# Recurrent stage of a pre-norm decoder layer: output projection of batches two to four as three rounded products of halves in place of fp32 matmuls

## The reference, cut to what matters

```python
def _min_gru(x, Wz, bz, Wh, bh):
    k = x @ Wz + bz
    log_z = -jax.nn.softplus(-k)
    log_coeffs = -jax.nn.softplus(k)
    log_tilde_h = _log_g(x @ Wh + bh)
    a_star = jnp.cumsum(log_coeffs, axis=1)
    log_h = a_star + _logcumsumexp(log_z + log_tilde_h - a_star, axis=1)
    return jnp.exp(log_h)
out_fwd = _min_gru(x, Wz_f, bz_f, Wh_f, bh_f)
out_bwd = _min_gru(x_rev, Wz_b, bz_b, Wh_b, bh_b)
concat = jnp.concatenate([out_fwd, out_bwd], axis=2)
return concat @ W_out + b_out
...
x = x + _L0_attn_ref(_layernorm(x, axis=-1), ...)
x = x + _L0_xattn_ref(_layernorm(x, axis=-1), ctx_1024, ...)
x = x + _L0_ffn_ref(_layernorm(x, axis=-1), ...)
```

## Time and profile before

| what | value |
|---|---|
| median of 3 runs | 404.35 us (404.19 to 405.8) |
| profiled execution, span | 403.8 us |
| profiled execution, its own time | the page gives none beside the span; the lowest timed run is 404.19 us |
| instructions | 7801 |
| PE busy | 395.0 us, 98% |
| DVE busy | 300.1 us, 74% |
| ACT busy | 237.8 us, 59% |
| POOL busy | 215.9 us, 53% |
| output projection | from 29.84 us (first batch) to 93.6 us (last batch) |

### The profile page before, as it was taken

One profiled execution on the slowest core, in us unless ns is written; L12 is line 12 of the kernel. 1 busy time (PEld: TensorE's weight loads), 2 busy tenths in 40 slices (PEclk: granted clock), 3 DMA queues, 4 the chain that ended last, 5 costly groups with the idle time before them and its releaser, 6 DMA issues.

```text
span 403.8 us, 7801 instructions
## 1 busy us (share of the span) xinstructions
PE 395.0 (98%) x2584; PEld 367.1 (91%) x2584; DVE 300.1 (74%) x1093; ACT 237.8 (59%) x519; POOL 215.9 (53%) x209
## 2 busy tenths in 40 slices
PE   8999999999999999999999999999999999999877
PEld 7878888899999999999999999999788899999766
DVE  5797768786757867476864848572986989899996
ACT  3886859454764466464545434342557977779462
POOL 1788999764385333153430300000166858989993
PEclk9999999999999999999999999999999969999999
DMA  7900213004434312233211000000100000000102
GB/s 226 310 2 1 83 55 102 8 11 128 128 89 121 118 30 59 58 84 104 65 47 30 2 0 2 1 2 2 27 1 2 0 2 2 28 28 27 41 28 67
DMA packets 19992, 21.38 MB, mean 53 GB/s; under 512 B 3180, under 2 KB 16624, under 8 KB 19952
## 3 DMA queue, kind: packets, MB, share of 16 engines
q1 hardware_dynamic: 18832, 19.96, 16.5%
q10 hardware_dynamic: 1120, 0.92, 0.7%
HBM read 18.78 MB, written 2.10 MB: 52 GB/s over the span
## 4 chain that ended last, share of the span: by engine, by line
PE 80%; POOL 12%; DVE 4%; issue 3%; DMA 1%; ACT 0%; SPq 0%; DVEq 0%; POOLq 0%; ACTq 0%
PE keep_pQ L75 11%; PE keep_pQ L76 11%; PE keep_pQ L77 11%; POOL ffn_prod L1258 9%; PE context_pA L1051 6%; PE context_pA L1053 6%; PE context_pA L1052 6%; PE context_pR L1085 6%; PE context_pR L533 3%; PE context_pA L533 3%; POOL ffn_near L1326 2%; PE ffn_pK L1807 2%; PE context_pR L75 2%; PE context_pR L77 2%; PE context_pR L76 2%
## 5 line engine op out<-in xcount | busy, mean ns | idle before, releaser
L899 DVE TENSOR_TENSOR att_pTl<-context_pR,att_pTh 128x512 fp32r<-128x512 f32 x64 | 36.9, 586 | 29.8 <-ACT att_pTh L811 29.5
L811 ACT ACTIVATE att_pTh<-context_pR 128x512 fp32r<-128x512 f32 x64 | 32.1, 514 | 40.1 <-PE context_pR L1085 40.1
L1258 POOL TENSOR_TENSOR ffn_prod<-ffn_first,ffn_near 128x1024 f32<-128x1024 f32 (+1 forms) x29 | 54.1, 1885 | 2.1 <-DVE ffn_first L1684 2.1
L851 ACT ACTIVATE att_prob<-keep_pQ,att_nmax 128x1206 f32<-128x1206 f32 x16 | 20.3, 1269 | 35.9 <-DVE att_nmax L935 35.8
L930 DVE TENSOR_REDUCE att_mx<-keep_pQ 128x1 f32<-128x402 f32 x64 | 34.5, 564 | 6.9 <-PE keep_pQ L77 6.6
L1837 PE MATMUL ffn_pT<-keep_ident,ffn_prod 128*128 128x128 f32 x240 | 30.5, 283 | 3.7 <-POOL ffn_prod L1258 3.7
L1837 PEld LDWEIGHTS ffn_pT<-keep_ident,ffn_prod 128*128 128x128 f32 x240 | 28.6, 148 | 5.8 <-DVE ffn_hT L1717 4.8
L786 POOL TENSOR_TENSOR keep_rstd<-att_ve,keep_mhalf 128x4 f32<-128x4 f32 x3 | 3.0, 1007 | 55.9 <-DVE att_ve L989 55.9
L1085 PE MATMUL context_pR<-keep_ident,att_prob 128*128 128x128 f32 (+1 forms) x208 | 31.8, 272 | 0.2 <-DVE att_pTl L899 0.2
L1051 PE MATMUL context_pA<-att_pTh,att_cNh 128*128 128x256 f32 (+1 forms) x104 | 31.0, 298 | 0.0
L1051 PE MATMUL context_pA<-att_pTh,context_cNh 128*128 128x256 f32 (+1 forms) x104 | 30.9, 297 | 0.0
(11 more groups left out here) (336 smaller groups left out, 1300.3 us busy)
## 6 DMA issues: line engine op xcount, KB each, us to landing
keep_raw<-in_ctxT SPq DMA_DIRECT2D x24, 256.0 KB, 2.7
keep_raw<-in_ctx SPq DMA_DIRECT2D x24, 256.0 KB, 3.0
out<-keep_x SPq DMA_DIRECT2D x16, 128.0 KB, 1.7
keep_x<-in_x SPq DMA_DIRECT2D x3, 512.0 KB, 9.9
gru_wout<-in_W_out SPq DMA_DIRECT2D x1, 512.0 KB, 8.7
keep_raw<-in_fWq SPq DMA_DIRECT2D x2, 256.0 KB
keep_raw<-in_ctxT SPq DMA_DIRECT2D x8, 32.5 KB, 3.1
keep_raw<-in_ctx SPq DMA_DIRECT2D x4, 65.0 KB
```

The lines of the kernel that those rows point to most:

```text
L811: act.activation(to, bank, ACT.Copy).then_inc(bank_high, 1)
L899: dve.tensor_tensor(to, bank, half(it, 0, n)[0].bitcast(F32), ALU.subtract).then_inc(bank_free, 1)
L1258: return eng.tensor_tensor(prod[:, i % PB, a:b].rearrange("p h (i j) -> p h i j", j=KEYS), (factor if factor is not None else first[:, n % ...
```

## The change

The output projection of the first batch stays in fp32. Those of batches two to four are made of halves. `state_high` (ACT) rounds each unit's state into `hh[b]`, `state_low` (DVE) subtracts in place (`hTl` lies over `hT`), and `halved_output` makes twelve products for a tile in place of four fp32 matmuls. W_out is halved once, at unit 6 on ACT and unit 7 on DVE, in place too, behind the first batch's four tiles. The tiles of batches two and three move one projection later; the fourth of batch two goes behind the first projection of batch four, and the fourth of batch three behind the last projection, next to the third. The copies of units 4 to 12 stand behind the second sigmoid two units on, the others where the diff shows them. `hh` of batches two and four lies over the gate weights and over `xn`.

```diff
+    hh1, wouth = beneath(hh1=[P, UNITS, SEQ], wouth=[P, UNITS, D])
...
+    hh3, = beneath(hh3=[P, UNITS, SEQ])
     xn = st.sb("xn", [P, 2, TPB, D])
+    woutl, = beneath(woutl=[P, UNITS, D])
     wout = st.sb("wout", [P, 2 * DC, D])
...
+    hTl, = beneath(hTl=[P, 2, UNITS, SEQ])
     hT = st.sb("hT", [P, 2, 2 * DC, SEQ])
...
+    hh = [None, hh1, st.sb("hh2", [P, UNITS, SEQ], F32R), hh3]
...
+    def state_high(act, m):
+        b, u = m // UNITS, m % UNITS
+        act.wait_ge(h_ready, m + 1)
+        if b == 1:
+            act.wait_ge(wl_pool, 2)
+            act.wait_ge(wl_dve, 2)
+        if b == BATCH - 1:
+            act.wait_ge(xT_mm, BATCH)
+        act.activation(hh[b][:, u], hT[:, b % 2, u], ACT.Copy).then_inc(hh_ready, 1)
+
+    def state_low(dve, m):
+        b, u = m // UNITS, m % UNITS
+        dve.wait_ge(hh_ready, m - UNITS + 1)
+        dve.tensor_tensor(hTl[:, b % 2, u], hT[:, b % 2, u], hh[b][:, u].bitcast(F32), ALU.subtract)\
+            .then_inc(hl_ready, 1)
+
+    def halved_output(pe, b, t):
+        cols, out = slice(t * P, (t + 1) * P), pOs[t // 2][:, t % 2]
+        if t == 0:
+            pe.wait_ge(hl_ready, UNITS * b - 1)
+        for k in range(UNITS):
+            if t == 0 and k == UNITS - 1:
+                pe.wait_ge(hh_ready, UNITS * b)
+            pe.matmul(out, hh[b][:, k, cols], wouth[:, k], start=(k == 0), stop=False)
+            pe.matmul(out, hh[b][:, k, cols], woutl[:, k], start=False, stop=False)
+            if t == 0 and k == UNITS - 1:
+                pe.wait_ge(hl_ready, UNITS * b)
+            last = pe.matmul(out, hTl[:, b % 2, k, cols], wouth[:, k], start=False, stop=(k == UNITS - 1))
+        return last
...
                 if n == LASTU:
+                    state_high(act, n - 2)
...
+                if UNITS + 2 <= n < LASTU:
+                    state_high(act, n - 2)
...
                 if n == 2 * UNITS - 2:
                     high(2)
+                    act.wait_ge(prep_mm, 1)
+                    act.wait_ge(ld_wout, 16)
+                    act.activation(wouth[:], wout[:], ACT.Copy).then_inc(wout_high, 1)
...
                 if n in HALVED:
                     low(b + 1)
+                if n == 2 * UNITS - 1:
+                    state_low(dve, n - 3)
                 if n == LASTU:
                     residual(BATCH - 2, 0)
+                    state_low(dve, n - 2)
...
                     candidate(n)
+                if n == 2 * UNITS:
+                    state_low(dve, n - 2)
                 if n >= 1 and n != UNITS:
                     scan((n - 1) // UNITS, (n - 1) % UNITS)
+                if n == 2 * UNITS - 1 or b >= 2 and u >= 2 and n < LASTU:
+                    state_low(dve, n - 2)
+                if n == 2 * UNITS - 1:
+                    dve.wait_ge(wout_high, 1)
+                    dve.wait_ge(out_mm, TPB)
+                    dve.tensor_tensor(woutl[:], wout[:], wouth[:].bitcast(F32), ALU.subtract).then_inc(wout_low, 1)
...
                     residual(b - 2, 1)
+                    if b == BATCH - 1:
+                        state_low(dve, n - 2)
+                    state_low(dve, n - 1)
                     if b - 2 < LEFT:
                         new_moments(b - 2)
         residual(BATCH - 2, 1)
+        state_low(dve, LASTU - 1)
         scan(BATCH - 1, UNITS - 1)
...
-            if t == 0:
-                pe.wait_ge(h_ready, UNITS * (b + 1))
...
+            if t == 0 and b == 1:
+                pe.wait_ge(wout_low, 1)
             if t % 2 == 0 and b >= 1:
                 pe.wait_ge(x2_ready, 2 * b - 1 + t // 2)
+            if b >= 1:
+                halved_output(pe, b, t).then_inc(out_mm, 1)
+                return
...
-                if j >= UNITS and b >= 1:
+                if j >= UNITS and b == 1:
                     output(b - 1, j - UNITS)
+                if j > UNITS and b >= 2:
+                    output(b - 1, j - UNITS - 1)
+                if j == 0 and b == BATCH - 1:
+                    output(b - 2, TPB - 1)
+                if j == 2 * UNITS - 1 and b == BATCH - 1:
+                    output(b - 1, TPB - 1)
...
         act.wait_ge(gru["offset_ready"], LASTB + 1)
+        act.wait_ge(gru["out_mm"], TPB * 2)
...
+        for m in range(BATCH * UNITS - 2, BATCH * UNITS):
+            gru["state_high"](act, m)
...
+                if g == 0 and j == 1:
+                    gru["state_low"](dve, BATCH * UNITS - 1)
...
-            pe.wait_ge(gru["h_ready"], BATCH * UNITS)
             pe.wait_ge(gru["x2_ready"], 2 * LASTB - 1 + t // 2)
...
+            gru["output"](pe, LASTB, t).then_inc(gru["out_mm"], 1)
```

More of the change, by code:

```diff
@@ L98, in stage_gru, with beneath @@
     ZB = 3
+    UNITS = 2 * DC
+    def beneath(**shapes):
+        with ExitStack() as late:
+            over = Stage(nc, late, "gru_over")
+            return [over.sb(n, shape, F32R) for n, shape in shapes.items()]
+    hh1, wouth = beneath(hh1=[P, UNITS, SEQ], wouth=[P, UNITS, D])
     w = st.sb("w", [P, 4, DC, D])
@@ L144, in stage_gru @@
     piece_hi, piece_lo, pad_set = st.sem("piece_hi"), st.sem("piece_lo"), st.sem("pad_set")
+    hh_ready, hl_ready, wout_high, wout_low = (st.sem(n) for n in ("hh_ready", "hl_ready", "wout_high", "wout_low"))
     pieces = context_pieces(d, keep, 0)
+    def state_high(act, m):
[25 more added lines that the diff above has]
+        return last
     keep["gru"] = {"gates": gates, "g_ready": g_ready, "h_ready": h_ready, "xb_ready": xb_ready, "out_mm": out_mm,
                    "x2_ready": x2_ready, "q0_low": q0_low, "piece_lo": piece_lo, "pad_set": pad_set,
-                   "offset_ready": offset_ready, "rstd": rstd, "offset": offset, "hT": hT, "wout": wout, "pO": pOs}
+                   "offset_ready": offset_ready, "rstd": rstd, "offset": offset, "pO": pOs,
+                   "state_high": state_high, "state_low": state_low, "output": halved_output}
     FIRST = 6
@@ L151, in stage_gru @@
     LASTU = BATCH * 2 * DC - 1
-    UNITS = 2 * DC
     DENSE = 13
@@ L524, in output @@
         def output(b, t):
-            if t == 0:
-                pe.wait_ge(h_ready, UNITS * (b + 1))
-                if b == 0:
-                    pe.wait_ge(ld_wout, 16)
-                    pe.wait_ge(prep_lo, 1)
+            if t == 0 and b == 0:
+                pe.wait_ge(h_ready, UNITS)
+                pe.wait_ge(ld_wout, 16)
+                pe.wait_ge(prep_lo, 1)
+            if t == 0 and b == 1:
+                pe.wait_ge(wout_low, 1)
             if t % 2 == 0 and b >= 1:
                 pe.wait_ge(x2_ready, 2 * b - 1 + t // 2)
+            if b >= 1:
+                halved_output(pe, b, t).then_inc(out_mm, 1)
+                return
             for k in range(2 * DC):
@@ L671, in stage_attention @@
     xn = st.sb("xn", [P, TPB, D])
+    qT1 = [st.sb(n, [P, DC, SEQ], F32R) for n in ("qT1h", "qT1l")]
     prob = st.sb("prob", [P, 2, CTX])
@@ L680, in stage_attention @@
     ve, rstd, ve3 = (st.sb(n, [P, TILES]) for n in ("ve", "rstd", "ve3"))
-    qT1 = [st.sb(n, [P, DC, SEQ], F32R) for n in ("qT1h", "qT1l")]
     qT = (qT0, qT1)
@@ L1006, in last_output @@
         def last_output(t):
-            pe.wait_ge(gru["h_ready"], BATCH * UNITS)
             pe.wait_ge(gru["x2_ready"], 2 * LASTB - 1 + t // 2)
-            for k in range(UNITS):
-                last = pe.matmul(gru["pO"][t // 2][:, t % 2], gru["hT"][:, LASTB % 2, k, t * P:(t + 1) * P],
-                                 gru["wout"][:, k], start=(k == 0), stop=(k == UNITS - 1))
-            last.then_inc(gru["out_mm"], 1)
+            gru["output"](pe, LASTB, t).then_inc(gru["out_mm"], 1)
         def scores(g):
```

## The result

The changed kernel takes 407.61 us (407.50 to 409.03, 5 runs); before, in the same comparison, 404.35 us (404.19 to 405.80, 5 runs). The ratio is 1.0076, with a 95% interval of 1.0056 to 1.0095: slower by 3.3 us. The forecast was 407.0 us, slower.

The account below looks back on a forecast made before the run. It took PE's chain as the bound, with POOL also full and locked against DVE; PE's 3.95 us saving was outweighed by added DVE and ACT work, last outputs 2.6 us late: 404.35 + 2.6 = 407.0 us, range 402 to 410.

Parts of the forecast that it names:

- walk: Recurrent stage, added instructions put into each queue in program order: last outputs end 96.2, before 93.62, +2.6 us; chance 0.46.
- rival A: All added work is hidden and PE's saving alone counts: 404.35 - 3.95 = 400.4 us; chance 0.14.
- Rival D: Output tiles: the products are dearer, at 0.18 us each, a loss of 5.6 us, up to 410; chance 0.03.
- Step 1: Unit 7: POOL's product ends 48.4, before 46.8; its scan 50.6, before 48.6; subtraction 7 ends 52.55; nothing hides this.
- Step 2: After subtraction 7 come the moments, waiting for POOL; candidate 9 starts 55.5, before 52.74; PE waits 0.8 us.
- Step 3: Fourth normalisation: offset 60.4, second half ends 65.45, before 62.07; PE stands 2.2 us, transposes end 66.4, before 64.42.
- Step 4: Subtractions 10 and 11 ahead of the moments end 74.35; low half of xT 5.8 us late, first queries 1.6 late.
- Step 5: Stage's end: scan 15 ends 90.2, before 86.1; first last tile 92.05, last outputs 96.2, before 93.62: +2.6 us.
- Rival C: Granted clock falls while PE stands 2.2 us ahead of the fourth transposes: about 409 us; chance 0.08.
- lock: Two-SBUF-input DVE instructions and POOL's exclude each other; the first holds it throughout; a subtraction adds 0.53 us, the wide one 1.07.
- POOL's sum: Ahead of the last scan: added 6.9 us where POOL has 5.15 left, so that scan ends 1.75 us after 86.1.
- Rival B: Added instructions take time in their own queues but don't lock POOL: last outputs end 92.8, 403.5 us; chance 0.15.

Follow-up runs that it names:

- Copies alone: Changed kernel without the subtractions of the state and of W_out; ACT's rounding copies stay and the twelve products read high halves: 401.70 us.
- last batch: Changed kernel with only the last batch's projection made of halves, the first three batches fp32 in their old places: 406.72 us.
- last two: Changed kernel with only batches three and four made of halves, W_out's subtraction at unit 10: 407.10 us.
- moments first: Changed kernel with the second norm's moments ahead of subtractions 7, 10 and 11, and the output tiles later on PE: 410.17 us.
- one-input twice: Kernel with one-input DVE operations for the subtractions, each behind a second one-input operation of the same length: 410.45 us.
- two products: Changed kernel without the state's subtractions and low-half products, eight products per tile: 401.95 us with ACT's copies, 401.73 us with the scan writing the rounded state.
- one-input: Changed kernel with each subtraction, of the state and of W_out, replaced by a DVE operation reading one operand, same output and waits: 402.75 us.
- the kernel without the wide subtraction: Changed kernel without W_out's subtraction; the high half is read in place of its low half: 407.52 us.
- the filled kernel: Kernel with only the last batch made of halves, plus 14 more products ahead of its first output tile, where PE stood: 406.48 us.
- products alone: Changed kernel whose scan writes the rounded state itself: no state copies, no subtractions, all twelve products take high halves: 401.30 us.

## Why the prediction was right, and where not

The time, sign and range were right (407.0 for 407.61; walk's outputs' end 96.2 for 97.17, or 96.8 without the 0.35 of the start). By its steps:

- *PE's saving*: 3.95 us, nearly right. Products take 0.12 us, so a tile takes 1.44 and saves 0.29, twelve tiles 3.5, and the kernel with only the products takes 401.30 where rival A said 400.4. (Rival D's price was reckoned a little high: at 0.18 us twelve products are 2.16, 0.43 above a tile of 1.73, so twelve tiles lose 5.2 us, not 5.6. It changes nothing.)
- *ACT*: the path of copy 9 and of the copy after scan 15 were named, and ACT's total (+7.0 us on the page) is a little under 8.5. Copies alone cost little, 0.4 us of the median.
- *Step 1*: POOL's product of unit 7 ends at 49.07 (48.4), scan 7 at 51.30 (50.6), subtraction 7 at 53.21 (52.55). Late by 0.7, of which the start has 0.35.
- *Step 2*: candidate 9 at 55.92 (55.5), right.
- *Step 3*: offset 60.76 (60.4), second half of the normalisation 65.78 (65.45), PE's pause 1.8 us (2.2), right.
- *Step 4*: subtractions 10 and 11 end at 74.86 (74.35), PE waits 1.5 us for the first of them (1.45), the low half of xT ends at 78.54 (78.0), right.
- *Step 5*: scan 15 ends at 90.77 (90.2), its subtraction 92.42 (91.85), the first last tile 92.85 (92.05), the last 97.17 (96.2). Here 0.4 us came on top: the last product of the first tile came 0.43 us after the release, and each of three tiles 1.44 us, for 1.40.
- *Rival C*, the clock: no fall in the changed kernel, though PE was busy for only 0.74 of the 2.50 us from 63.5 on. Behind pauses in four relatives of it (last batch, last two, moments first, one-input twice) it fell, behind a longer one in "two products" it didn't. The chance of 0.08 was for a thing that happens in near relatives of this kernel, and that no fall came here is in part luck. The row it was taken from also had eight matmuls 128 wide among the narrow ones.

**The lock as the cause** stands: with it taken away (one-input) 5.45 us of the loss go, and the walk, which let each subtraction wait for POOL and each POOL instruction for a subtraction, had the dates. Taking away the wide subtraction alone gave 1.0 us, where the prediction priced it at 1.07. POOL's product takes 2.29 us under the wide subtraction.

What doesn't stand as written is the **step from POOL's sum to the date**. The sum has the right size: over the whole run, with the same 209 instructions, POOL is busy 223.3 us, against 215.9 before and 216.2 to 217.0 in the six kernels that don't subtract the state (one-input twice among them: 216.3). That is 6.3 to 7.4 us more, where 6.9 were reckoned ahead of the last scan and 0.53 behind it. But "POOL has 5.15 us left, so the last scan must come 1.75 late" names one of two full queues. DVE had 12.1 us left in the earlier trace rows, and I took this as cover. The one-input kernel doubled doesn't lengthen POOL's products and loses at least as much as the change. DVE's cover is not its idle sum but what of it lies ahead of a candidate: subtraction 7 and the moments stand in one queue before candidate 9, and PE, ACT and POOL all wait for that. The walk kept that order in its steps 2 and 4, the sum didn't; the time came from the walk.

Rival B took unlocked subtractions at 0.66 and 1.2 us, 9.1 us in all, and said 403.5 (0.85 us faster than before); the one-input kernel, with just that DVE time, was 2.2 us faster. So B's sum was 1.3 us too high for its premise, and its premise didn't hold here.

In all, each against before on its own chip: products alone -3.6 us, copies +0.4, DVE work of one-input length +1.05, the subtractions' two operands, with the waiting that these bring, +5.45; sum +3.3.

## What to carry to other kernels

A saving on the full engine is worth its time only as long as the engine that feeds it isn't asked for more: count the feeder's free time per stage and ahead of its own critical instruction, not over the stretch (here the first 9.2 of 12.1 us cost about 1, the next 6.6 cost 5.45). When a change loses, don't shrink it before you know which queue loses: one third of this one, two thirds and a reordering were all slower than before. When you compare dates of two traces, first subtract what they are apart ahead of the change, and when times fall into groups by the granted clock, compare like groups: without this the kernel without the wide subtraction looked as if nothing had been gained. With the state's low half left out (two products) the kernel was 2.9 to 3.1 us faster than before, and the next bound was a transfer released by POOL.

## What the runs showed of the hardware

- A granted clock below full appeared behind four short stretches in which PE was busy for 1.29 of 3.00, 1.07 of 3.00, 0.01 of 3.00 and 1.50 of 3.00 us; the 4 us behind them had 0.57 to 0.61 ("last batch": 17 products at 0.21 us, some 1.5 us lost). After 0.74 of 2.50 us busy in the changed kernel and 0.30 of 3.00 in "two products" there was none. So a pause of PE alone doesn't bring the fall.
- One kernel's executions lie in groups: before on one chip six at 404.09 to 404.88 us with a mean granted clock of 1.000 and six at 405.83 to 406.68 with 0.992; the filled kernel near 405.1, 406.5 and 408.0. A single profiled execution can be 3 us off its kernel's best.
- A subtraction of two SBUF operands on DVE takes 0.66 to 0.68 us when it starts ahead of POOL's instruction and up to 1.78 when it doesn't; POOL's 128x512 products, 1.27 to 1.30 us beside a one-input operation, take 1.72 to 2.29 beside it. The wide one (1.20 us in one-input form) takes 2.32.
- Even an operation of DVE on four columns takes part in this: 0.16 us alone, 1.33 behind an instruction of POOL. Whether it is met decides 1.1 us between two executions of the same code.
